# A four-layer graph network on one core: three sets of loads and stores split at row 96, one fill moved, one normalization moved to ScalarE

## What is computed

```python
x = _layernorm(x + L0(x, edge_weight, src, dst, ...))  # relu([h[src], h[dst], w] @ W1 + b1) @ W2 + b2, segment_max over dst,
                                                       # then relu([h, agg] @ U1 + c1) @ U2 + c2
x = _layernorm(x + L1(x, factors, src, dst, ...))      # relu([x[src], factors[dst]] @ Wm + bm), segment_sum, relu([x, agg] @ Wc + bc)
x = _layernorm(x + L2(x, src, dst, ...))               # four attention heads of 32: softmax over the edges of each dst, weighted sum
x = _layernorm(x + L3(x, src, dst, ...))               # two rounds: mean of x[src] over dst, x @ W[0] + mean @ W[1], relu between them
```

## Time and profile before

| what | value |
|---|---|
| time, median of 3 runs | 5681.93 us (5680.7 to 5690.96) |
| profiled execution | 5663.14 us, span 5661.4 us |
| busy share of the span | POOL 64%, PE 55%, PEld 41%, DVE 40%, ACT 22% |
| GpSimd's gathers and scatters of rows | about 0.95 us each, 1.25 us from one to the next |
| bytes moved | 1015.34 MB, mean 179 GB/s |

### The profile page before, as it was taken

How to read it: one execution, slowest core, us unless ns; L and a number is a source line. 1 busy time by engine, 2 the same in 40 slices (tenths; PEclk the granted TensorE clock), 3 DMA queues, 4 the chain that set the end, 5 groups by cost and what they waited for, 6 DMA issues and landing times. The chain is left out here.

```text
span 5661.4 us, 75437 instructions
## 1 busy us (share of the span) xinstructions
PE 3112.8 (55%) x16332; PEld 2315.0 (41%) x16332; DVE 2254.2 (40%) x4035; ACT 1224.2 (22%) x2253; POOL 3637.8 (64%) x3813
## 2 busy tenths in 40 slices
PE   1368888887488885455454533333333533333345
PEld 0345555554366664344453432333333323333333
DVE  2124444444477763455554563222222222222224
ACT  0112222222144442222232321111111211111111
POOL 3277777776601105777777766777777777777776
PEclk9579999998799997777777765555555655555557
DMA  6879999998299984334343433444444334444443
GB/s 232 307 230 303 304 304 300 300 305 276 86 311 326 326 305 89 96 104 112 102 114 102 112 96 113 129 135 127 136 128 134 115 124 135 129 135 127 136 128 104
DMA packets 693883, 1015.34 MB, mean 179 GB/s; under 512 B 145813, under 2 KB 395258, under 8 KB 683722
## 3 DMA queue, kind: packets, MB, share of 16 engines
q1 hardware_dynamic: 372248, 485.42, 25.9%
q0 software_dynamic: 134688, 301.60, 20.4%
q10 hardware_dynamic: 186780, 226.46, 11.1%
HBM read 580.47 MB, written 433.03 MB: 179 GB/s over the span
## 5 line engine op out<-in xcount | busy, mean ns | idle before, releaser
L1359 POOL DMA_INDIRECT gath<-sender_table,src_cols x1664 | 1569.9, 943 | 574.0 <-issue 504.4
L1399 PE MATMUL bank<-ident,gath 128*128 128x128 f32 x1664 | 464.1, 434 | 1277.7 <-DMA gath<-sender_table,src_cols 1277.7
L1632 POOL DMA_INDIRECT gath<-attention_table,src_cols x832 | 809.4, 973 | 262.9 <-issue 190.5
L1156 POOL DMA_INDIRECT gath<-joint_table,src_cols x832 | 788.6, 948 | 261.5 <-issue 188.3
L1399 PEld LDWEIGHTS bank<-ident,gath 128*128 128x128 f32 x1664 | 297.7, 217 | 1443.7 <-DMA gath<-sender_table,src_cols 1443.7
L1425 ACT ACTIVATE rows<-bank 128x512 f32<-128x512 f32 x416 | 248.1, 597 | 1849.5 <-PE bank L1409 1849.5
L784 POOL DMA_INDIRECT gath<-scan_rows,end_i x147 | 140.5, 955 | 569.7 <-ACTq L1559 525.8
L1331 DVE TENSOR_TENSOR_SCAN scan<-meta,scan,bank 128x512 f32<-128x512 bf16 x208 | 266.2, 1280 | 372.1 <-DVEq L1328 360.9
L1442 DVE TENSOR_TENSOR_SCAN scan<-over_head,den,bank 128x512 f32<-128x512 bf16 x104 | 133.1, 1280 | 480.7 <-PE bank L1399 480.7
L1442 DVE TENSOR_TENSOR_SCAN den<-over_head,scan,bank 128x512 f32<-128x512 bf16 x104 | 133.1, 1280 | 421.2 <-PE bank L1399 421.2
L1895 DVE TENSOR_TENSOR_SCAN scan<-bank,scan,hid 128x512 f32<-128x512 f32 x208 | 266.3, 1280 | 79.3 <-DVEq L1894 75.6
(11 more groups left out here) (269 smaller groups left out, 5907.3 us busy)
## 6 DMA issues: line engine op xcount, KB each, us to landing
scan_rows<-rows SPq DMA_DIRECT2D x624, 256.0 KB
recv<-receiver_rows SPq DMA_DIRECT2D x416, 256.0 KB
attention_scan_rows<-rows ACTq DMA_DIRECT2D x208, 264.0 KB
receiver_rows<-gath ACTq DMA_DIRECT2D x26, 2048.0 KB, 17.4
factor_rows<-gath ACTq DMA_DIRECT2D x208, 256.0 KB
scan_rows<-rows ACTq DMA_DIRECT2D x208, 256.0 KB
gath<-factor_rows SPq DMA_DIRECT2D x208, 256.0 KB
over_head<-edge_meta SPq DMA_DIRECT2D x52, 1024.0 KB
```

The lines of the kernel that those rows point to most:

```text
L1156: pool.indirect_dma_start(out=landed[s][:, c, 0:width], out_offset=None, in_=table[:, :], in_offset=bass.IndirectOffsetOnAxis(ap=src_cols[ ...
L1359: pool.indirect_dma_start(out=gath[s][:, c, 0:F], out_offset=None, in_=table[:, :], in_offset=bass.IndirectOffsetOnAxis(ap=src_cols[:, t:t ...
L1399: ins = pe.transpose(b[:, c * P:(c + 1) * P], gath[s][:, c, 0:F], ident[:, :])
L1632: pool.indirect_dma_start(out=gath[s][:, c, :], out_offset=None, in_=att_d[:, :], in_offset=bass.IndirectOffsetOnAxis(ap=src_cols[:, t:t + ...
```

## The change

Three edits:

1. Transfers over 103, 104 or 106 rows are issued as one over rows 0 to 95 and one over the rest (`EVEN` = 96): the loads of `dst`, `prev_r` and `src`, the 62 rows of the last column of `first_dst` (48 and 14), the floats of `dst`, the marks, the last rows of `x`, of the factors and of the output. The loads of `src` move behind those of `prev_r`. `START_TURN` goes from 8 to 6.
2. The zeros of `scan_rows` are issued amid node stage 0, behind the stores of group 4 (`NG // 3`).
3. In node stage 3 VectorE makes `scale` = 1/std and `shift` = -mean/std for each tile, and ScalarE writes the normalized rows as `scale * y + shift` (`scaled_rows`, four ACTIVATEs for a group). A semaphore tells VectorE when ScalarE has read `y_nm`. The four multiplications by the heads' sums become one instruction.

```diff
@@ preparation, SyncE's queue
-                    for r, t in ((dst_r, a["dst"]), (src_r, a["src"])):
-                        sp.dma_start(flat(r)[0:PP - 1, :], t[0:E - left]...).then_inc(loaded, 16)
-                        sp.dma_start(flat(r)[PP - 1:PP, 0:left], t[E - left:E]...).then_inc(loaded, 16)
+                    for lo, hi in ((0, EVEN), (EVEN, PP - 1)):
+                        sp.dma_start(flat(dst_r)[lo:hi, :], a["dst"][lo * run:hi * run]...).then_inc(loaded, 16)
+                    sp.dma_start(flat(dst_r)[PP - 1:PP, 0:left], a["dst"][E - left:E]...).then_inc(loaded, 16)
...
-                    sp.dma_start(dst_d..., flat(dst_f)[0:PP, :]).then_inc(dst_written, 16)
+                    for lo, hi in ((0, EVEN), (EVEN, PP)):
+                        sp.dma_start(dst_d...[lo:hi, :], flat(dst_f)[lo:hi, :]).then_inc(dst_written, 16)
...
-                    sp.dma_start(x_nm[0:N - whole * P, whole, :], a["x"][whole * P:N, :]).then_inc(n_load, 16)
+                    for lo, hi in ((0, EVEN), (EVEN, N - whole * P)):
+                        sp.dma_start(x_nm[lo:hi, whole, :], a["x"][whole * P + lo:whole * P + hi, :]).then_inc(n_load, 16)
...
-START_TURN = 8
+START_TURN = 6
@@ node stage, SyncE's queue
+                def clear_scan(q, s):
+                    if 2 * q + s == NG // 3:
+                        sp.dma_start(scan_d[EP - CLEARED[1] * EB:EP, :].rearrange("(p r) f -> p r f", p=P),
+                                     zero_c[:, :].unsqueeze(1).to_broadcast([P, CLEARED[1] * CT, F])).then_inc(cleared, 16)
...
-                if k == 0:
-                    sp.dma_start(scan_d[EP - CLEARED[1] * EB:EP, :]...).then_inc(cleared, 16)
@@ node stage, VectorE
-                        for c in range(w):
-                            ins = v.tensor_tensor(o[:, c, :]..., from_rows[:, c, :]..., h[:, c, :]..., ALU.mult)
-                            ins.then_inc(v_done, 1)
+                        chain(v.tensor_tensor(o.rearrange("p c (h d) -> p c h d", h=HEADS), from_rows.rearrange("p c (h d) -> p c h d", h=HEADS),
+                                              h.unsqueeze(3).to_broadcast([P, w, HEADS, HID]), ALU.mult))
...
                     elif k == 3:
+                        if q > 0:
+
+                            v.wait_ge(n_y_free, 1)
+                            v.sem_inc(n_y_free, -1)
                         chain(v.tensor_tensor(y, x, agg[s][:, 0:w, :], ALU.add))
...
+                    if k == 3:
+                        chain(v.reciprocal(scale[s][:, 0:w], std[s][:, 0:w]))
+                        v.scalar_tensor_tensor(shift[s][:, 0:w], mv[s][:, 0:w, 0], -1.0, scale[s][:, 0:w], ALU.mult, ALU.mult).then_inc(n_scale, 1)
+                        return
@@ node stage, ScalarE
+                def scaled_rows(q, s):
+                    w = GROUP_TILES[2 * q + s]
+                    x, y = x_nm[:, tiles(q, s), :], y_nm[s][:, 0:w, :]
+
+                    act.wait_ge(n_scale, 1)
+                    act.sem_inc(n_scale, -1)
+                    for c in range(w):
+                        act.activation(x[:, c, :], y[:, c, :], ACT.Identity, bias=shift[s][:, c:c + 1], scale=scale[s][:, c:c + 1]).then_inc(a_done, 1)
+                    act.wait_ge(a_done, w)
+                    act.sem_inc(a_done, -w)
+                    act.sem_inc(n_x, 1)
+                    act.sem_inc(n_tab, 1)
+                    if 2 * q + s + 2 < NG:
+                        act.sem_inc(n_y_free, 1)
```

More of the change, by code:

```diff
@@ L33 @@
 PP = T // TQ
-assert T % TQ == 0 and 96 < PP <= P
+EVEN = PP // 16 * 16
+assert T % TQ == 0 and 96 == EVEN < PP <= P
 NG = -(-N // EB)
@@ L181, in gnn_program @@
         stats = sb("stats", [P, CT, 6]); mv = [sb(f"mv{s}", [P, CT, 2]) for s in range(2)]; std = [sb(f"std{s}", [P, CT]) for s in range(2)]; rstd = sb("rstd", [P, CT])
+        scale = [sb(f"scale{s}", [P, CT]) for s in range(2)]; shift = [sb(f"shift{s}", [P, CT]) for s in range(2)]
         head_sum = sb("head_sum", [P, CT * HEADS])
@@ L205, in gnn_program @@
         n_std = sem("n_std")
+        n_scale = sem("n_scale"); n_y_free = sem("n_y_free")
         n_x = sem("n_x")
@@ L671, in turn @@
                     def turn(q, s):
-                        pe.wait_ge(fac_in[s], 16)
-                        pe.sem_inc(fac_in[s], -16)
-                        t = fac_last if isinstance(q, int) and q * SLOTS + s == NG - 1 else recv[s]
+                        last = isinstance(q, int) and q * SLOTS + s == NG - 1
+                        pe.wait_ge(fac_in[s], 32 if last else 16)
+                        pe.sem_inc(fac_in[s], -32 if last else -16)
+                        t = fac_last if last else recv[s]
                         for c in range(CT):
@@ L834, in store_out @@
                     if whole < CT and N % P:
[L835 to L837 removed]
+                        for lo, hi in ((0, EVEN), (EVEN, N % P)):
+                            sp.dma_start(out[N - N % P + lo:N - N % P + hi, :], x_nm[lo:hi, N // P, :]).then_inc(out_done, 16)
+                def clear_scan(q, s):
+                    if 2 * q + s == NG // 3:
+                        sp.dma_start(scan_d[EP - CLEARED[1] * EB:EP, :].rearrange("(p r) f -> p r f", p=P),
+                                     zero_c[:, :].unsqueeze(1).to_broadcast([P, CLEARED[1] * CT, F])).then_inc(cleared, 16)
+                work = [(0, store_table)] * (to_d is not None) + [(0, store_receivers)] * makes_recv + [(0, store_out)] * (k == 5) + [(0, clear_scan)] * (k == 0)
                 if k == 1:
@@ L1061, in table @@
                     act.sem_inc(n_heads if k == 2 else n_tab, 1)
-                work = ([(new + 2, table)] * (w_tab is not None) + [(new + 1, turned_x)] * turn + [(late, deviation)] * norm
+                work = ([(new + 2, table)] * (w_tab is not None) + [(new + 1, turned_x)] * turn + [(late + 1, scaled_rows)] * (k == 3) + [(late, deviation)] * norm
                         + [(1, hidden), (0, keep_aggT)] * dense)
```

61 lines of the change are left out of this document (31 added, 30 removed).

## The result

| kernel | median us | runs | ratio to before, 95% interval |
|---|---|---|---|
| before | 5681.32 | 5678.27 to 5690.96 (4) | |
| after | 5615.12 | 5610.56 to 5615.93 (4) | 0.9879, 0.9862 to 0.9896 |

The change takes 66.2 us, 1.2%. The forecast was 5613 us, between 5595 and 5634. The profiled execution of after took 5615.93 us (span 5614.2), 0.8 us above its median; that of before took 5663.14, 18 us under its median of four (18.8 under that of the three runs that the prediction had). So the two traces differ by 47 us and the medians by 66, and the sum of the prediction, made for the traces, was 69.

The account below looks back on a forecast made before the run. It took one-engine loads, then DMA work, to bound the preparation, GpSimd node stage 0 and VectorE node stage 3. Edits 1 to 3 give 52 + 0 + 17 = 69 us off 5681.9: 5613 us, range 5595 to 5634.

Parts of the forecast that it names:

- rival B: Preparation: late gathers make TensorE wait for start_f and ScalarE's fills run dry; up to 12 us, 5625; chance 0.10.
- the 2.8 us assumed for a block's end with no DMA waited for: End of node stage 0: idle time left of 8.3 us once the fill moves, so up to 5.5 us gained.
- the wait amid the stage: Node stage 0: stores behind the moved fill make GpSimd's scatter of group 7 slip 6 us.
- The hop at the end: End of node stage 3: passing the last normalizing to ScalarE costs 0.4 us of the 17.3 gained.
- I take that as the same for both kernels: Whole kernel: the median stands 18.8 us above the profiled execution, before and after the change alike.
- A: Moved fill in node stage 0 gains (5607) or loses 8 us (5621); counted inside the forecast's 0.83.
- C: Preparation: the split does nothing, loads still stand behind the fills; only edit 3 counts, 5665 us; chance 0.04.
- D: Node stage 0: moved fill holds SyncE's queue far longer; slower by 0.2% from about 99 us of holding; chance 0.01.

Follow-up runs that it names:

- e1: After with edit 1 undone (nothing split, old order, START_TURN 8): 5655.71 us, ratio 0.9974 to before.
- e4: The kernel before, unchanged, profiled once more: 5684.88 us in one execution.
- e10: After with nothing split; of edit 1 only src behind prev_r and START_TURN 6 stay: span 5654.7 us, one execution.
- e2: After with the fill of scan_rows back behind all stores of node stage 0: 5602.03 us, ratio 0.9882 to before.
- e3: After with VectorE normalizing again and multiplying tile by tile (edit 3 undone): 5621.10 us, ratio 0.9911 to before.
- e5: After once more, with no edit: 5601.59 us, ratio 0.9878 to before.
- e6: After with the fill of scan_rows in four pieces of 1 MB behind the stores of groups 2 to 5: 5602.97 us, ratio 0.9881 to before.
- e9: After with START_TURN back at 8: span 5602.3 us, one execution.
- e12: After with the fill of scan_rows in eight pieces of 0.5 MB behind the stores of groups 1 to 8: 5595.81 us, one execution.
- e11: After with ScalarE's zero fills held until VectorE's loads land, dst split at row 102 and src unsplit: span 5620.2 us, one execution.
- e7: After with dst and src split at row 102 in place of 96: span 5600.8 us, one execution.

## Why the prediction was right, and where it wasn't

**Edit 1, forecast 52 us.** Right. Between the profiles with no split and those with all of them the first matmul falls from 247.4 (four: before, e1, e4, e10) to 198.1 us (seven: after, e2, e3, e5, e6, e9, e12), 49.3 us. That the splits do it, and not the order, is shown by e10. The reading of 0.06 as one engine of sixteen is shown by e11. VectorE's start came at 22.8 (22 forecast), and 6 us more of it cost nothing (e7), because the stage is bound by what the DMA engines have to move: each share times its window adds up to 189 us of all engines in before, to 247 us, and to 186 in after, to 197. The working by shares and bytes held within 3 us. Two of its times on the way were off without harm. The trip of `dst_rows` through DRAM ended 20 us behind its issue (26.4 us), where it had been 7.5 (85.4 to 92.9); it now stands among the fills, at a DMA share of 1.03 in that stretch, where before had 0.50. GpSimd started at 46.5 us, so `start_f` came at 133 us, not 116. That is the condition of rival B. Its price was shown to be nothing by e9: ScalarE was two steps of fills ahead.

**Edit 2, forecast 0, between -5.5 and +8.** The stage became 4.4 us longer (92.4 on the mean of nine profiles, 88.0 of three), within the bounds. The value taken failed at two terms of the sum. What could be gained at the end was 8.30 - 5.61 = 2.7 us, not 5.5: the 2.8 us assumed for a block's end with no DMA waited for stand in no row of the prediction and in no run, and they are 5.61 here. And the wait amid the stage was 4.9 us ahead of group 7 (6 forecast) and another 2.4 ahead of group 5, which was not foreseen: the sum priced the stores behind the fill, and not the scatters beside it.

**Edit 3, forecast 17.** It gave 16.1 us (119.7 to 103.6, means of three and eleven profiles). The step fell by 1.51 us (1.44 forecast), so twelve by 18.1. The hop at the end cost more than the 0.4 us put down for it: from VectorE's last aggregate to the mean sweep's first gather (3377.85) 6.9 us pass, where it had been 4.4 (to 3424.43). VectorE's end of that stage in before, then in after:

```profile
3420.01 0.18 DVE L935 BATCH_NORM_AGGREGATE mv<-stats 128x2 f32<-128x6 f32 x1 [0.50 <-DVEq L933]
```

```profile
3370.99 0.18 DVE L953 BATCH_NORM_AGGREGATE mv<-stats 128x2 f32<-128x6 f32 x1
3372.71 0.16 DVE L962 RECIPROCAL scale<-std 128x1 f32<-128x1 f32 x1 [1.53 <-DVEq L960]
3373.02 0.16 DVE L963 SCALAR_TENSOR_TENSOR shift<-mv,scale 128x1 f32<-128x1 f32 x1
```

**The sum, and the step that failed.** The three stretches give 49.3 - 4.4 + 16.1 = 61.0 us where 69 were forecast. The comparisons of times give 66 and 67, with 59 to 79 as their interval, which holds both sums. The step that was wrong is "I take that as the same for both kernels": the 18.8 us between before's profiled execution and its median are no fixed part of an execution. Before's profiled execution had a short joint sweep (1059.9 us, where e4 has 1077.4 and the four profiles without splits 1069.9 on the mean), and after's had a long one (1072.0) and stood at its median. The sweep accounts for some 10 of the 18.8 us; what the other 8 or 9 were isn't shown, but the medians of one kernel differ by as much between comparisons (5681 and 5671). So the profiled time forecast by the sum, 5594, was missed by 22 us, of which 12 are this sweep, 3 the rest, and 6 the terms (69 against 50.3 - 3.9 + 16.2 = 62.6 in these two traces), while the median was met. That the forecast of the median is within 3 us of the measured one owes something to chance: the terms were 8 us too large, and 5 us of the measured gain stand in none of the three stretches.

What stays open is why the joint sweep varies, and whether it became shorter on the mean. The four profiles without splits have 1069.9 us (1059.9 to 1077.4), the ten with splits in the inputs 1062.3 (1057.7 to 1072.0). That would account for the 5 or 6 us between 61 and the measured 66 and 67, but the two ranges overlap, and nothing in the sweep was changed by an experiment.

**The rivals.** A came out as a loss of 4.4 us, inside its bounds. B's condition came true and its price was nought (e9). C is refuted by the start at 22.8 us: the splits took 49 us off. The rule "Don't bother" on two transfers to disjoint partition halves, in the Trainium skill, "DMA: Bandwidth & Descriptors", section "Rules for kernel authors", gives as its reason that both halves use all 16 engines; it doesn't carry over to this case, where the unsplit load of 103 rows ran at a share of 0.06. The rule on the divisor of the row count, in the Trainium skill, "DMA: Bandwidth & Descriptors", section "Why a DMA increments its semaphore by 16 and not by 1", agrees with e11 for 102 rows (6 engines) and 103 (1). D: the queue was held for 14.9 us, far under 99.

## What to carry to other kernels

Where a load is alone, as in e11, a low and constant DMA share can be read as a count of engines: 0.06 was one of sixteen, 0.35 to 0.41 were six. Look for a transfer whose row count has no large divisor, split off its rest, and then price the gain by what the DMA engines must move in the stage in any case, not by the start that comes earlier. A large fill on a queue that serves small stores is worth cutting into pieces, each shorter than the slack of the store behind it; here that made the stage 6.7 us shorter in one profile, and no comparison of times shows it.

Before a sum is made against one profiled execution, find out in which stage executions of the same kernel differ; a second profile of the kernel before shows it.

## What the runs showed beyond that

- The wait ahead of a store behind one DMA of 4 MB was 14.86 us on SyncE's queue, behind pieces of 1 MB 2.3 to 4.0 and of 0.5 MB 0.4 to 2.2 us. The queue itself, not only the engines, is what a large DMA occupied here; whether it goes by bytes or by the number of runs wasn't tested.
- Four ACTIVATEs over 128 words with scale and bias per partition take 1.65 us, 0.48 each and 0.39 from one to the next, where 1.2 to 2.3 had been left open.
- In the joint sweep GpSimd's pace is the same in every profile (832 gathers in 1041 to 1044 us), and yet the sweep takes 1058 to 1077 us, since its gathers don't wait for the engines that use them. In this sweep the engine that looks like the pace isn't what ends it.
